# Opening of a two-layer perceiver kernel: second-layer weight loads moved behind the first keys, three casts moved from VectorE to ScalarE

## The reference, cut to what matters

```python
# L0 cross attention, 16 heads of 16 channels
xn = layernorm(x)                         # 256 x 256
q = (xn @ Wq.T + bq)                      # 256 x 256
k = (ctx @ Wk.T + bk)                     # 4096 x 256
v = (ctx @ Wv.T + bv)                     # 4096 x 256
scores = q @ k.T per head                 # 16 x 256 x 4096
# a temperature per head comes from statistics of the scores,
# then softmax, times v, times Wo, added to x
```

## Time and profile before

| what | us |
|---|---|
| median of 3 runs | 1378.09 |
| lowest and highest run | 1377.07, 1380.81 |
| the profiled execution, its own time | 1383.17 |
| its span | 1381.4 |
| PE busy | 1127.1 (82%) |
| ACT busy | 893.1 (65%) |
| DVE busy | 823.8 (60%) |
| POOL busy | 630.4 (46%) |
| block a ends, block b's first matmul | 49.8, 51.2 |

### The profile page before, as it was taken

The page is one execution under the profiler, slowest core; times in us unless marked ns, Lnnn a source line. Parts: engine busy times, 40 slices in busy tenths (PEclk is TensorE's granted clock), DMA queues, the critical chain, the costliest instruction groups (busy, mean ns, idle before and its releaser), DMA issues. The chain is left out here.

```text
span 1381.4 us, 25688 instructions
## 1 busy us (share of the span) xinstructions
PE 1127.1 (82%) x8423; PEld 692.4 (50%) x8423; DVE 823.8 (60%) x1510; ACT 893.1 (65%) x1206; POOL 630.4 (46%) x293
## 2 busy tenths in 40 slices
PE   7687877757999858989977778888888888858798
PEld 3343444433444436678862444544444444434687
DVE  6688888871110176562235787888878887945312
ACT  3599999976989724533322787888888888624110
POOL 2177778760000005000002888899999999900000
PEclk9799999987999968899995899999999999977899
DMA  7875545537555062014467888999989989534130
GB/s 251 241 225 124 130 108 134 126 92 152 112 110 107 0 197 75 1 49 153 152 220 244 322 311 303 303 325 328 325 313 326 319 319 337 192 98 141 46 137 8
DMA packets 97048, 257.51 MB, mean 186 GB/s; under 512 B 11193, under 2 KB 41305, under 8 KB 85466
## 3 DMA queue, kind: packets, MB, share of 16 engines
q1 hardware_dynamic: 96992, 256.79, 59.5%
HBM read 165.31 MB, written 91.92 MB: 186 GB/s over the span
## 5 line engine op out<-in xcount | busy, mean ns | idle before, releaser
L1934 POOL TENSOR_TENSOR xb_row<-xb_row,w_mask 128x1024 f32<-128x1024 f32 x128 | 419.1, 3286 | 241.0 <-DVE xb_row L1964 239.4
L1964 DVE TENSOR_TENSOR xb_row<-xb_cont_ps,xb_row 128x1024 f32<-128x1024 f32 x128 | 156.7, 1224 | 86.9 <-PE xb_cont_ps L1757 67.4
L1757 PE MATMUL xb_rel_ps<-xb_kk,xb_qq 32*128 32x512 f32 x496 | 147.9, 674 | 35.7 <-ACT xb_out L1882 33.8
L554 DVE TENSOR_REDUCE xa_stats<-xa_b_ps 128x1 f32<-128x1024 f32 x128 | 155.8, 1220 | 33.4 <-PE xa_b_ps L470 32.7
L1975 DVE CUSTOM_DVE_ANT_0 xb_row<-xb_row,xb_minus 128x1024 f32<-128x1024 f32 x128 | 171.8, 1342 | 0.0
L1887 ACT ACTIVATE xb_row<-xb_row,xb_ntop 128x2048 f32<-128x2048 f32 x64 | 128.3, 2005 | 56.4 <-DVE xb_ntop L1981 56.4
L1757 PE MATMUL xb_cont_ps<-xb_kk,xb_qq 32*128 32x512 f32 x528 | 157.9, 676 | 2.8 <-DVE xb_row L1964 1.7
L864 ACT ACTIVATE xa_probs<-xa_psT,xa_t_now 128x1024 f32<-128x1024 f32 x128 | 141.1, 1114 | 20.3 <-PE xa_psT L823 20.1
L1882 ACT COPY xb_out<-xb_rel_ps 128x1024 f32<-128x1024 f32 x124 | 124.8, 1006 | 40.5 <-PE xb_rel_ps L1757 25.2
L522 ACT ACTIVATE xa_exps<-xa_b_ps,xa_stats 128x1024 f32<-128x1024 f32 x128 | 141.3, 1108 | 14.0 <-DVE xa_stats L554 14.0
L1801 PEld LDWEIGHTS xb_turn_ps<-_ident,xb_row 128*128 128x128 f32 x1008 | 115.9, 148 | 55.1 <-issue 55.1
(11 more groups left out here) (367 smaller groups left out, 1832.7 us busy)
## 6 DMA issues: line engine op xcount, KB each, us to landing
xb_row<-rel_scores SPq DMA_DIRECT2D x128, 512.0 KB, 6.6
rel_scores<-xb_out SPq DMA_DIRECT2D x32, 1024.5 KB, 6.0
rel_scores<-xb_out SPq DMA_DIRECT2D x32, 1024.0 KB, 5.9
b_e_w<-in_L_ffn_e_w SPq DMA_DIRECT2D x32, 513.0 KB, 3.5
w_w<-in_L_ffn_w SPq DMA_DIRECT2D x24, 512.0 KB, 4.8
xa_k<-first_parts SPq DMA_DIRECT2D x24, 384.0 KB, 5.0
value_rows<-xa_values SPq DMA_DIRECT2D x16, 544.0 KB, 6.1
xb_kk<-key_blocks SPq DMA_DIRECT2D x17, 512.0 KB, 8.1
```

The lines of the kernel that those rows point to most:

```text
L554: nc.vector.tensor_reduce(stats[:, c % 2, 0, u:u + 1], ps[:, slot % 4], AX, ALU.min).then_inc(s["min_ready"], 1)
L1757: mm = nc.tensor.matmul(out[:, k * BANK:(k + 1) * BANK], qq[rows, b, kind, t * P:(t + 1) * P], kk[rows, b, half], start=True, stop=True)
L1934: nc.gpsimd.tensor_tensor(row[:, held(c), at:at + SUB], row[:, held(c), at:at + SUB], mask[:, t, half * HALF + at:half * HALF + at + SUB], ...
L1964: nc.vector.tensor_tensor(row[:, held(c), at:at + SUB], cont_ps[:], row[:, held(c), at:at + SUB], ALU.add).then_inc(s["cont_out"], 1)
```

## The change

The eight weight loads on SP's queue move from ahead of the stores to behind the loads of the first keys. `rest` becomes two buffers, used in turns. For groups 1, 3 and 5 the cast to part 1 is made by ScalarE, after it has evacuated the next group; VectorE makes the next group's first remainder before it subtracts for part 2 of such a group. ScalarE now may write `whole` again once the first remainder has been made from it.

```diff
--- before.py
+++ after.py
@@ -234,9 +234,12 @@
 
 
         with ExitStack() as inner:
+            rest_odd = f.sb(inner, "rest_odd", [P, QUARTER])
+            ACT_CASTS = (1, 3, 5)
+            rest_of = lambda n: (rest, rest_odd)[n % 2]
             s = {n: f.sem("a_" + n) for n in ("x_loaded", "q_w_loaded", "k_w_loaded", "var_ready", "root_ready", "dve_steps",
                                               "xn_ready", "xnT_mm", "xnT_sb", "q_mm", "q_read", "q_split", "projected",
-                                              "evacuated", "rest_done", "second_done", "split_done", "ones_set")}
+                                              "evacuated", "rest_done", "second_done", "second_cast", "split_done", "ones_set")}
             ctx_loaded = [f.sem(f"a_ctx_loaded{g}") for g in range(NQU)]
             block = inner.enter_context(nc.Block())
             ps = f.ps(inner, "a_ps", [P, 4, QUARTER])
@@ -259,14 +262,6 @@
                 sp.wait_ge(parts_stored, 48)
                 load_first_queries(f, sp, q96, q_loaded)
 
-                for n, name in enumerate(("L1_xattn_Wk", "L1_xattn_Wp")):
-                    sp.dma_start(wk[:, 1 + n], rows_of(i[name])).then_inc(later_loaded, 16)
-                for n, name in enumerate(("L1_xattn_bk", "L1_xattn_bp")):
-                    sp.dma_start(bcol[:, 1 + n], i[name]).then_inc(later_loaded, 16)
-                for m in range(2):
-                    for t in range(KC):
-                        sp.dma_start(wv[:, m * KC + t], rows_of(i[f"L{m}_xattn_Wv"])[:, :, t * P:(t + 1) * P]
-                                     ).then_inc(later_loaded, 16)
                 for n, (g, t) in enumerate(key_groups):
                     sp.wait_ge(s["split_done"], n + 1)
                     dst = f.first_parts[:, t * P:(t + 1) * P, g * QUARTER:(g + 1) * QUARTER]
@@ -276,6 +271,14 @@
                             sp.wait_ge(stored[b], 16)
                         for h in range(2):
                             load_first_keys(f, sp, k96[0:ROWS, h], h, k_loaded[h])
+                        for n, name in enumerate(("L1_xattn_Wk", "L1_xattn_Wp")):
+                            sp.dma_start(wk[:, 1 + n], rows_of(i[name])).then_inc(later_loaded, 16)
+                        for n, name in enumerate(("L1_xattn_bk", "L1_xattn_bp")):
+                            sp.dma_start(bcol[:, 1 + n], i[name]).then_inc(later_loaded, 16)
+                        for m in range(2):
+                            for t in range(KC):
+                                sp.dma_start(wv[:, m * KC + t], rows_of(i[f"L{m}_xattn_Wv"])[:, :, t * P:(t + 1) * P]
+                                             ).then_inc(later_loaded, 16)
                 sp.wait_ge(q_loaded, 96)
 
             @block.tensor
@@ -320,7 +323,7 @@
                 for n, (g, t) in enumerate(key_groups):
                     act.wait_ge(s["projected"], n + 1)
                     if n >= 2:
-                        act.wait_ge(s["split_done"], n - 1)
+                        act.wait_ge(s["rest_done"], n - 1)
                     if n >= 4:
                         act.wait_ge(stored[n % 4], 16 * (n // 4))
 
@@ -328,6 +331,9 @@
                                          accum_out=f.key_sums[:, t, g:g + 1])
                     nc.scalar.activation(parts[:, n % 4, 0], ps[:, (n + 2) % 4], ACT.Identity,
                                          bias=bcol[:, 0, t:t + 1]).then_inc(s["evacuated"], 1)
+                    if n - 1 in ACT_CASTS:
+                        act.wait_ge(s["rest_done"], n)
+                        nc.scalar.copy(parts[:, (n - 1) % 4, 1], rest_of(n - 1)[:]).then_inc(s["second_cast"], 1)
 
             @block.vector
             def _(dve):
@@ -348,17 +354,32 @@
                 step(nc.vector.tensor_tensor(qparts[:, 2], qrest[:], qparts[:, 1], ALU.subtract))
                 dve.sem_inc(s["q_split"], 1)
                 step(nc.vector.tensor_reduce(q_sums[:], q[:], AX, ALU.add))
+                def first_rest(n):
+                    dve.wait_ge(s["evacuated"], n + 1)
+                    if n >= 2:
+                        dve.wait_ge(s["split_done"], n - 1)
+                    nc.vector.tensor_tensor(rest_of(n)[:], whole[:, n % 2], parts[:, n % 4, 0], ALU.subtract
+                                            ).then_inc(s["rest_done"], 1)
+
+                def second(n):
+                    dve.wait_ge(s["rest_done"], n + 1)
+                    nc.vector.tensor_copy(parts[:, n % 4, 1], rest_of(n)[:]).then_inc(s["second_done"], 1)
+
+                def third(n):
+                    if n in ACT_CASTS:
+                        dve.wait_ge(s["second_cast"], ACT_CASTS.index(n) + 1)
+                    else:
+                        dve.wait_ge(s["second_done"], n + 1 - sum(k < n for k in ACT_CASTS))
+                    nc.vector.tensor_tensor(parts[:, n % 4, 2], rest_of(n)[:], parts[:, n % 4, 1], ALU.subtract
+                                            ).then_inc(s["split_done"], 1)
+
                 for n in range(len(key_groups)):
-                    dve.wait_ge(s["evacuated"], n + 1)
-                    if n >= 1:
-                        dve.wait_ge(s["split_done"], n)
-                    nc.vector.tensor_tensor(rest[:], whole[:, n % 2], parts[:, n % 4, 0], ALU.subtract
-                                            ).then_inc(s["rest_done"], 1)
-                    dve.wait_ge(s["rest_done"], n + 1)
-                    nc.vector.tensor_copy(parts[:, n % 4, 1], rest[:]).then_inc(s["second_done"], 1)
-                    dve.wait_ge(s["second_done"], n + 1)
-                    nc.vector.tensor_tensor(parts[:, n % 4, 2], rest[:], parts[:, n % 4, 1], ALU.subtract
-                                            ).then_inc(s["split_done"], 1)
+                    first_rest(n)
+                    if n - 1 in ACT_CASTS:
+                        third(n - 1)
+                    if n not in ACT_CASTS:
+                        second(n)
+                        third(n)
```

## The result

| | before | changed |
|---|---|---|
| median of 12 runs, us | 1376.03 | 1385.20 |
| lowest and highest | 1371.58, 1380.81 | 1373.57, 1389.16 |
| ratio, 95% interval | | 1.0051 (1.0029 to 1.0072) |
| profiled execution, own time and span | 1383.17, 1381.4 | 1389.16, 1387.4 |

The change makes the kernel slower by 0.5%, 7.0 us of 1376, and the interval (4.0 to 9.9 us) begins beside the 4.1 us that was forecast. The two medians lie further apart, 9.2 us, because the changed kernel's runs fall into two groups: four at 1373.57 to 1376.83 us with a mean granted clock of 0.930 to 0.938, and eight at 1382.97 to 1389.16 us with 0.922 to 0.928. The means are 7.1 us apart. With nine more runs the median of before is 1376.03; the three that stood ahead of the prediction had 1378.09, and the profiled execution, at 1383.17, lies above all twelve.

The account below looks back on a forecast made before the run. The opening's DMA transfers were taken to set the time, not VectorE and ScalarE. First keys 0.9 us later plus 3.2 us of weights made +4.1 us on 1378.09, so 1382.2 us, range 1378.0 to 1385.0.

Parts of the forecast that it names:

- The mechanism: In the opening, transfers run in series, so later keys and weights behind them delay the next block; +4.1 us, chance 0.62.
- The second chain: The opening's transfers, ending 11 us after VectorE and ScalarE finish at 49.8 us, set when the next block gets on.
- the sum: Opening's total: first keys 0.9 us later plus 3.2 us of weights, +4.1 us, carried to the kernel's end.
- the fourth store: Key-part store before the first keys: issued at 37.0 us, landing 4.3 us later at 41.3, so keys 0.9 us later.
- The walk through group 3's cast: Opening: ScalarE's cast behind the fifth evacuation, 34.4 to 35.5 us; VectorE's subtraction ends at 37.0 instead of 34.25.
- Block start: Next block: TensorE's first matmul waits for all weight loads, 56.2 us instead of 51.22; VectorE's first copy at 65.2.
- Weights beside the keys: Rival, opening: weights travel within the keys' half-rate stretch, leaving only +0.9 us, 1379.0; chance 0.10.
- The casts do no harm: Rival, opening: the fourth store goes as early as before, so only the weights' +3.2 us remain, 1381.3; chance 0.06.
- SP held: Rival, SP's queue: full behind the keys, it delays issuing the last stores; +6.4 to +7.5 us, chance 0.05.
- The clock: Rival, next block: TensorE's clock doesn't fall again, +2.3 us, chance 0.10; or longer idling costs, +5.9 us, 0.03.
- the likeliest of the three outcomes: Whole kernel: time within 0.3% of before, given 0.57, against 0.39 for slower and 0.04 for faster.

Follow-up runs that it names:

- casts alone: Kernel before, with three casts moved to ScalarE and the weight loads left ahead of the stores; ratio 1.0035 (1.0014 to 1.0056).
- early weights: Kernel before, with the eight weight loads moved up straight behind the context's loads, casts on VectorE; ratio 0.9992 (0.9973 to 1.0010).
- idle casts: Kernel before, with ScalarE also casting a constant tile three times into an unused one, nobody waiting; ratio 0.9996 (0.9977 to 1.0015).
- the repeat: The changed kernel profiled and timed again without any edit; ratio to before 1.0046 (1.0028 to 1.0063).
- the 768 KB: Changed kernel, with 768 KB of the same weights loaded once more into a spare tile behind the first 1 MB; ratio 1.0054 (1.0035 to 1.0073).
- two casts: Changed kernel, with group 3's cast back on VectorE, so ScalarE casts groups 1 and 5 only; ratio 1.0031 (1.0010 to 1.0053).
- early release: Changed kernel, with SP raising keys_stored and values_stored ahead of its wait for the eight stores; ratio to before 1.0014 (0.9994 to 1.0034).

## Why the prediction was right, and where it was off

**The mechanism holds.** The second chain, the transfers, sets the time. From the first keys' issue to the first copy it takes 19.1 to 20.7 us in the five kernels with the store wait and no weights between (the two profiles of before, casts alone, early weights, idle casts; mean 19.8), and 23.1 to 23.4 in the four with them. So the weights cost 3.5 us of a full stretch, against 3.2 in the sum.

**Moving the weights frees time and the casts use it up.** The prediction had this as one step, a first-keys issue 0.9 us later. It is -2.5 us (37.80 against 40.3) for the stores that are ready sooner and +2.5 us for the casts. The sum is 0.0 in the repeat. The term that was mis-sized is the fourth store: issued at 36.6, not 37.0, it was ready for the keys 3.7 us later, not 4.3. In the first profile the keys went at 41.36, as forecast (41.3), by luck: the context was 0.8 us late, about what the fourth store was forecast too late. The walk through group 3's cast holds as it stands, 18.3 us from the first evacuation's start to the end of group 3's subtraction in both profiles of the changed kernel, against 18.4 in the prediction.

**Block start.** The forecast was 56.2 for the first matmul and 65.2 for the copy; 56.62 and 64.59 in the first profile (context 0.8 us late), 55.46 and 63.52 in the repeat. VectorE ended the opening at 48.47 in the repeat, 1.3 us sooner than 49.80 (forecast 0.7), and it was hidden under the transfers, as said.

**Rivals.** Weights beside the keys: refuted by the stretch of 3.7 us and by the 768 KB. The casts do no harm: refuted by the pair with and without them. SP held: it is, 6.0 us for four stores that take 0.45 us each, but TensorE waits for the weights until after that, so it shows no price here; with the 768 KB more the block starts with the barrier, at 58.2, though the first copy still waits 1.67 us for the stores behind that. The clock: the low clock stayed away, as this rival supposes, but gave back nothing. TensorE's second idle time shrank from 2.6 to 0.7 us (forecast 1.8). Before, the granted clock fell after it to 0.50, from 63 to 69 us in the first profile and from 62 to 68 in the second; in the changed kernel it fell only from 68 to 71 us, and in the repeat it stayed at 1.00 from 59 to 76 us. Yet from the first copy to L746 it took 254.2 and 253.8 us before, and 255.2 and 254.4 us in the changed kernel: none of the 1.8 us came back. The longer idle time ahead of the block cost nothing more either, for VectorE got to the copy 6.7 and 6.2 us behind the block's first matmul, against 6.8 and 6.3 before.

**The size.** +4.1 us was forecast, +7.0 measured (4.0 to 9.9). The changed kernel's median, 1385.20, is a little above the 1385.0 at which the range ended, and the likeliest of the three outcomes had been no clear change. The marks account for +4.2 us: L746 at 318.8 in the mean of two profiles, against 314.7 in two of before (0.30%). That this is the sum to a tenth is luck in part: the first copy is 3.4 us late in the same mean, with the late context of the first profile in it, and the other 0.8 us come between it and L746, where the sum had nothing.

The rest of the 7.0 us is in no term of the sum. In three kernels with casts of real groups the timed ratio is above the mark's: 0.46 to 0.51% against 0.30% for the change, 0.35% against 0.11% for casts alone, 0.31% against 0.10% for two casts. In all others the two agree within 0.1%, and two of those have the casts as well (early release 0.14% and 0.06%, 768 KB more 0.54% and 0.55%). The profiles show where such time would lie: from L746 to the end of the span it takes 1063.7 to 1067.6 us in the six profiles with real casts on ScalarE, and 1055.8 to 1066.1 us in the eight others. But it is also longer the later L746 is (1055.8 us behind 311.20, 1067.6 us behind 319.77), and no run separates the two. The mean granted clock is lower in the timed runs of all with real casts (0.927 to 0.930; before 0.932 to 0.9335 beside the repeat and the experiments), also in the two that agree with their marks. Idle casts, with three casts on ScalarE and the extra buffer and semaphore, don't show it. It is two or three us on intervals of about three either way; whether it is real, and what makes it, stays open.

## What to carry to other kernels

Loads that are wanted only later belong where the DMA engines are idle, and idle time is seen in the DMA share by the microsecond, not in bytes. Behind a slow reload, with stores after them that gate the next block, 1.05 MB of them cost 3.5 us here. An engine with idle time can take a cast for nothing, but a cast that stands behind the next group's evacuation is a delay for whoever waits for it, so look at what hangs on that group's store, and at what the other engine does behind it. Ask too what slack a full queue hid: once the stores went early, a context 1.05 us late went with keys 1.04 us late, where before 1.06 us did not reach them. And ask of each semaphore raised after a wait whether it guards what is waited for.

## What the runs showed that I had not expected

- Two VectorE instructions that don't depend on each other start 1.15 us apart (35.30 and 36.45), where a dependent one starts 1.26 us after the same operation (20.88 and 22.14 before). Interleaving groups gives back a little of what it delays.
- SP can be held by one issue for 3.46 us behind the keys; without that, an issue of such a load took 0.43 to 0.47 us.
- The timed runs of one kernel spread over 13 us (before: 1369.04 to 1381.96 in 31 runs), and the time goes with the mean granted clock (0.94 at 1369, 0.926 at 1382). Marks in the profile resolve a change in the opening that 12 runs of the total barely do.
